# Attention probabilities packed at 80 columns a head, ten full tiles a chunk

## The reference, cut to what matters

```python
Q = (queries @ W_q.T).reshape(b, sq, 16, 16).transpose(0, 2, 1, 3)
K = (keys @ W_k.T).reshape(b, -1, 16, 16).transpose(0, 2, 1, 3)
V = (values @ W_v.T).reshape(b, -1, 16, 16).transpose(0, 2, 1, 3)
scores = jnp.einsum('bhqd,bhkd->bhqk', Q, K) / scale
scores = jnp.where(mask, scores, NEG_INF)
attention = jax.nn.softmax(scores, axis=-1)
heads_out = jnp.einsum('bhqk,bhkd->bhqd', attention, V)
out = heads_out.transpose(0, 2, 1, 3).reshape(b, sq, 256) @ W_proj.T + b_proj
```

## Time and profile before

| what | value |
|---|---|
| median of 3 executions | 1815.34 us (1811.38 to 1818.04) |
| span of the profiled execution | 1817.2 us; its own time beyond the span is not listed, and the three times lie on both sides of it |
| busy: PE, DVE, ACT, POOL | 1666.7, 1496.2, 889.4, 774.7 us (92, 82, 49, 43%) |
| mean granted PE clock | 0.981 of full |
| the 2048 matmuls of `x_av` | 246.2 us busy |
| the 1024 transposes of `prob` | 155.9 us busy |
| weight loads | issued in the first 21 us; ACT first uses the second half of them at 44.96 us |

### The profile page before, as it was taken

The page is one execution under the profiler, slowest core; times in us unless marked ns, Lnnn a source line. Parts: engine busy times, 40 slices in busy tenths (PEclk is TensorE's granted clock), DMA queues, the critical chain, the costliest instruction groups (busy, mean ns, idle before and its releaser), DMA issues.

```text
span 1817.2 us, 36129 instructions
## 1 busy us (share of the span) xinstructions
PE 1666.7 (92%) x12064; PEld 1497.1 (82%) x12064; DVE 1496.2 (82%) x3540; ACT 889.4 (49%) x2351; POOL 774.7 (43%) x809
## 2 busy tenths in 40 slices
PE   3699999999999999999999999999999999999986
PEld 3588888889888888888888988888888888898875
DVE  4778888888888888888888888888888888888652
ACT  2255544455554455555445555444555444555441
POOL 2344444444544444444444454444444444445320
PEclk9899999999999999999999999999999999999887
DMA  4000000000000000000000000000000000000000
GB/s 113 9 9 1 15 15 15 14 14 0 14 14 14 14 14 14 0 14 14 14 14 14 12 2 14 14 14 14 14 0 14 14 14 14 14 10 5 9 7 12
DMA packets 44572, 24.99 MB, mean 14 GB/s; under 512 B 24432, under 2 KB 44528, under 8 KB 44528
## 3 DMA queue, kind: packets, MB, share of 16 engines
q1 hardware_dynamic: 44528, 24.43, 5.1%
HBM read 16.03 MB, written 8.39 MB: 13 GB/s over the span
## 4 chain that ended last, share of the span: by engine, by line
PE 56%; DVE 30%; issue 9%; ACT 4%; DVEq 0%; DMA 0%; SPq 0%; POOL 0%; ACTq 0%; POOLq 0%
PE bank L377 49%; DVE a_conv L809 6%; PE bank L611 4%; DVE x_nmax L942 3%; DVE dve_scrap L252 2%; DVE a_xn L759 2%; PE bank L383 2%; DVE f_xn L759 2%; ACT x_prob L1211 2%; DVE a_E L792 1%; DVE a_stats L746 1%; DVE x_stats L746 1%; DVE f_s L1018 1%; DVE f_th L1013 1%; DVE x_xnT_lo L774 1%
## 5 line engine op out<-in xcount | busy, mean ns | idle before, releaser
L1211 ACT ACTIVATE x_prob<-bank,x_nmax 128x77 f32<-128x77 f32 x1024 | 247.7, 327 | 167.9 <-DVE x_nmax L942 163.7
L377 PEld LDWEIGHTS bank<-x_Vx,x_probT 77*128 77x128 f32 x2048 | 251.6, 193 | 2.9
L377 PE MATMUL bank<-x_Vx,x_probT 77*128 77x17 f32 x2048 | 246.2, 255 | 0.0
L1222 ACT ACTIVATE x_probT<-bank 77x512 f32<-77x512 f32 x256 | 152.4, 595 | 92.0 <-PE bank L611 92.0
L942 DVE TENSOR_REDUCE x_nmax<-bank 128x4 f32<-128x308 f32 x256 | 121.3, 474 | 59.8 <-PE bank L377 58.4
L611 PE MATMUL bank<-ident,x_prob 128*77 128x128 f32 x1024 | 155.9, 275 | 0.4 <-ACT x_probT L1222 0.4
L809 DVE SCALAR_TENSOR_TENSOR a_conv<-a_raw,cw,a_conv 128x256 f32<-128x256 f32 x384 | 156.2, 477 | 0.0
L1306 POOL TENSOR_TENSOR x_rstd<-x_ve,mhalf 128x2 f32<-128x2 f32 x32 | 22.6, 706 | 301.2 <-DVE x_ve L752 301.2
L1330 POOL TENSOR_TENSOR a_Er_lo<-a_E,a_Er_hi 128x512 fp32r<-128x512 f32 x32 | 74.2, 2320 | 142.2 <-ACT a_Er_hi L1114 142.2
L611 PEld LDWEIGHTS bank<-ident,x_prob 128*77 128x77 f32 x1024 | 124.0, 148 | 7.6 <-issue 0.6
L377 PE MATMUL bank<-x_K_bd,x_Q_stack 128*128 128x308 f32 x256 | 98.6, 385 | 15.0 <-ACT x_prob L1211 12.3
(11 more groups left out here) (250 smaller groups left out, 5585.2 us busy)
## 6 DMA issues: line engine op xcount, KB each, us to landing
x<-in_x SPq DMA_DIRECT2D x32, 256.0 KB, 2.9
out<-x SPq DMA_DIRECT2D x32, 256.0 KB, 2.2
ctxT<-in_ctxT SPq DMA_DIRECT2D x32, 77.0 KB, 2.5
keep<-in_mask SPq DMA_DIRECT2D x32, 19.2 KB, 2.6
f_s<-in_fWu SPq DMA_DIRECT2D x2, 256.0 KB, 5.6
a_AT<-in_Wv SPq DMA_DIRECT2D x1, 256.0 KB, 3.8
a_okn<-in_Ws SPq DMA_DIRECT2D x1, 256.0 KB, 3.9
a_qn<-in_Wg SPq DMA_DIRECT2D x1, 256.0 KB, 3.8
```

The costliest lines, as they stand in the source:

```text
L377: return pe.matmul(out, lhsT, rhs, start=start, stop=stop, skip_group_check=True)
L1211: ins = act.activation(prob[:, u % 2, i, :], X0[:, i * S2:(i + 1) * S2], ACT.Exp, scale=-1.0, bias=nmax[:, u % 2, i:i + 1])
L1222: act.activation(probT[:, u % 2].rearrange("p h t -> p (h t)"), X1[0:S2, :], ACT.Copy).then_inc(on.x_pT, 1)
```

## The change

`prob` becomes one tile for a whole chunk, [128, 1280]: 16 heads at a pitch of 80 columns, so that it is ten tiles of 128 columns. The last 3 columns of each head stay zero. A transpose now turns a full 128x128 tile, which holds parts of two or three heads. The ten tiles are done in four groups of 2, 3, 2 and 3, in the places of the four units of a chunk. `x_av` multiplies a transposed tile with a block layout of V, `Vbd`: for each tile up to 3 x 17 columns, a head's V rows standing at the partitions where that head's columns fell, zeros elsewhere. A head that is cut by a tile's edge is summed over two tiles in X2.

`Vbd` (two buffers, one for each row parity) is built from `Vtok`, the plain V that ACT's `x_v` writes, by DMAs from SBUF to SBUF, since rows must change partitions. SP's new step `spread_v` issues twelve a row: one for each piece of heads 0 to 7, with heads 8 to 15 (five tiles on) in the same DMA. The pieces are of 77, 48, 29, 77, 16, 61, 64, 13, 77, 32, 45 and 77 tokens, and each token of a piece is two runs of 64 bytes. `spread_v` waits for `x_v` and for the last `x_av` of the row two before; PE's `x_av` of unit 0 waits for all twelve (`vbd_in`). The zeros and ones of `Vbd` are loaded once, by two more DMAs in the list of the second weights.

The waits of `x_prob` and of the ACT step `x_pt` on PE are fitted to the new buffers.

```diff
+PITCH = 80
+NT = NH * PITCH // P
+GROUPS = (range(0, 2), range(2, 5), range(5, 7), range(7, 10))
+VW = 3 * (HD + 1)
...
-        Vx = sb("x_Vx", [S2, NH, HD + 1])
+        Vtok = sb("x_Vtok", [S2, NH, HD])
+        Vbd = [sb(f"x_Vbd_{i}", [P, NT, VW]) for i in range(2)]
-        prob = sb("x_prob", [P, 2, UH, S2])
-        probT = sb("x_probT", [S2, 2, UH, P])
+        prob = sb("x_prob", [P, NH * PITCH])
+        probT = sb("x_probT", [P, NT, P])
...
+        def pieces():
+
+            found = []
+            for h in range(NH // 2):
+                s = 0
+                while s < S2:
+                    t, p = divmod(h * PITCH + s, P)
+                    n = min(S2 - s, P - p)
+                    found.append((s, n, h, t, p, (h - first_head(t)) * (HD + 1)))
+                    s += n
+            return found
...
+            (Vbd[0][:], a["vones"]), (Vbd[1][:], a["vones"]),
...
+            def spread_v(r):
+                sp.wait_ge(on.x_v, upto(r))
+                if second(r):
+                    sp.wait_ge(on.x_av_ps, upto(two_before(r), NU))
+                dst, src = Vbd[r.parity], Vtok[:].rearrange("s (g h) e -> s g h e", g=2)
+                for s, n, h, t, p, col in V_PIECES:
+                    sp.dma_start(dst[p:p + n, t::NT // 2, col:col + HD], src[s:s + n, :, h, :]).then_inc(vbd_in, 16)
...
                     load_context(ra)
+                if rx is not None:
+                    spread_v(rx)
                 if rf is not None:
                     sp.wait_ge(on.f_y, upto(rf))
...
-                for i in range(UH):
-                    ins = pe.transpose(X1[0:S2, i * P:(i + 1) * P], prob[:, u % 2, i, :], ident[:])
+                for i, t in enumerate(GROUPS[u % QU]):
+                    ins = pe.transpose(X1[:, i * P:(i + 1) * P], prob[:, t * P:(t + 1) * P], ident[:])
...
                 if u == 0:
                     pe.wait_ge(on.x_v, upto(r))
+                    pe.wait_ge(vbd_in, upto(r, V_DMAS))
...
-                for i in range(UH):
-                    h = q * UH + i
-                    ins = mm(X2[:, h * (HD + 1):(h + 1) * (HD + 1)], probT[:, u % 2, i, :], Vx[:, h, :])
+                for t in GROUPS[q]:
+                    h, w = first_head(t) * (HD + 1), tile_heads(t) * (HD + 1)
+                    ins = mm(X2[:, h:h + w], probT[:, t, :], Vbd[r.parity][:, t, 0:w], start=(t == 0),
+                             stop=(t == NT - 1))
...
             def x_v(r):
                 if later(r):
-                    act.wait_ge(on.x_av_ps, upto(before(r), NU))
+                    act.wait_ge(vbd_in, upto(before(r), V_DMAS))
                 act.wait_ge(on.x_v_ps, upto(r))
-                act.activation(Vx[:, :, 0:HD], X2[0:S2, 0:D].rearrange("p (h e) -> p h e", h=NH), ACT.Copy).then_inc(on.x_v, 1)
+                act.activation(Vtok[:], X2[0:S2, 0:D].rearrange("p (h e) -> p h e", h=NH), ACT.Copy).then_inc(on.x_v, 1)
...
-                if u >= 2:
-                    act.wait_ge(on.x_pT_ps, upto(r, NU, u - 1))
+                last = min(q + 2, QU)
+                if c == 1:
+                    act.wait_ge(on.x_pT_ps, upto(r, NU, last))
...
-            pool.memset(Vx[:], 1.0).then_inc(z_ready, 1)
+            pool.memset(prob[:], 0.0).then_inc(z_ready, 1)
```

More of the change, by code:

```diff
@@ L219, in build @@
         st_y = [sem(f"st_y{i}") for i in range(2)]
+        vbd_in = sem("vbd_in")
         w_ready = sem("w_ready")
@@ L247, in loaded, with first_head, tile_heads @@
             return row.half * (16 * n) + 16 * n
+        def first_head(t):
+            return t * P // PITCH
+        def tile_heads(t):
+            return (t * P + P - 1) // PITCH + 1 - first_head(t)
+        def pieces():
[8 more added lines that the diff above has]
+            return found
+        V_PIECES = pieces()
+        V_DMAS = 16 * len(V_PIECES)
         def hold(eng, scrap):
@@ L365, in _ @@
             load_context(Row(last - 1, 1))
-            for rf in (Row(last - 2, 1), Row(last - 1, 0), Row(last - 1, 1)):
+            for rx, rf in ((Row(last - 1, 0), Row(last - 2, 1)), (Row(last - 1, 1), Row(last - 1, 0)),
+                           (None, Row(last - 1, 1))):
+                if rx is not None:
+                    spread_v(rx)
                 sp.wait_ge(on.f_y, upto(rf))
@@ L1204, in x_prob @@
                 act.wait_ge(on.x_max, upto(r, NU, u + 1))
-                if u >= 2:
-                    act.wait_ge(on.x_pT_ps, upto(r, NU, u - 1))
-                else:
-                    if later(r):
-                        act.wait_ge(on.x_pT_ps, upto(before(r), NU, NU - 1 + u))
+                c, q = divmod(u, QU)
+                last = min(q + 2, QU)
+                if c == 1:
+                    act.wait_ge(on.x_pT_ps, upto(r, NU, last))
+                elif later(r):
+                    act.wait_ge(on.x_pT_ps, upto(before(r), NU, QU + last))
                 for i in range(UH):
-                    ins = act.activation(prob[:, u % 2, i, :], X0[:, i * S2:(i + 1) * S2], ACT.Exp, scale=-1.0,
+                    col = (q * UH + i) * PITCH
+                    ins = act.activation(prob[:, col:col + S2], X0[:, i * S2:(i + 1) * S2], ACT.Exp, scale=-1.0,
                                          bias=nmax[:, u % 2, i:i + 1])
@@ L1216, in x_pt @@
                 act.wait_ge(on.x_pT_ps, upto(r, NU, u + 1))
[L1217 to L1222, removed]
+                if u >= QU:
+                    act.wait_ge(on.x_av_ps, upto(r, NU, u + 1 - QU))
+                elif later(r):
+                    act.wait_ge(on.x_av_ps, upto(before(r), NU, QU + u + 1))
+                g = GROUPS[u % QU]
+                act.activation(probT[:, g[0]:g[-1] + 1, :].rearrange("p h t -> p (h t)"), X1[:, 0:len(g) * P],
+                               ACT.Copy).then_inc(on.x_pT, 1)
             def x_ot(r):
@@ L1451, in constants, with ones_columns @@
         "iota8": np.tile(np.arange(NE, dtype=f32), (P, 1)),
+        "vones": ones_columns(),
     }
+def ones_columns():
+    vones = np.zeros((P, NT, VW), np.float32)
+    for h in range(NH):
+        for s in range(S2):
+            t, p = divmod(h * PITCH + s, P)
+            vones[p, t, (h - t * P // PITCH) * (HD + 1) + HD] = 1.0
+    return vones
 def kernel(**inputs):
@@ L1476 @@
     arrays = {f"in_{n}": np.ascontiguousarray(v) for n, v in arrays.items()}
-    nc = bacc.Bacc("TRN2", target_bir_lowering=False, num_devices=1)
+    nc = bacc.Bacc("TRN2", target_bir_lowering=False, num_devices=1, dynamic_dma_scratch_size=1024)
     aps = {n[3:]: nc.dram_tensor(n, v.shape, mybir.dt.from_np(v.dtype), kind="ExternalInput").ap()
```

## The result

The changed kernel took 2066.7 us (median of 4 runs, 2066.3 to 2067.87), the kernel before 1815.01 us beside it: a ratio of 1.139, with an interval of 1.137 to 1.141. I had forecast 1900 us, from 1810 to 1980. The sign and the kind of loss were right; the size was not. The profiled execution has a span of 2064.2 us, 247 us more than before, and a mean granted clock of 0.907 where there was 0.981.

What follows compares the result with a forecast made beforehand. PE bounds the kernel, with DVE leading each pass up to unit 5's scores. 29 full passes at +2.8 us (81) plus 3 for filling and draining took the 1817.2 us span to 1901, median 1900 us; range 1810 to 1980.

Steps and rivals of the forecast that it cites:

- The step that failed: SP's twelve V issues: 0.47 us apart (0.43 to 0.60), eleven steps 5.2 us, V complete at 856.0, PE stalled 3.6 us.
- The second term: PE's work behind unit 5's scores: fewer transposes and matmuls save 2.06 us a pass, and DVE can just follow.
- DVE's five waits: DVE's waits for PE, or ACT behind PE, after unit 5's scores start: 2.4 us, set against PE's saving of 2.06.
- the forecast's mechanism: V late at `x_av` 0; PE's gap drops the clock to 1.2 GHz each full pass, 6.8 us taken; chance 0.6.
- the forecast's +0.2: Full pass with the clock at full: the stall costs 2.25 us, the saving returns 2.06, so +0.2 us.
- my 2.8: Loss per full pass with 6.8 us of low clock: unit 5's scores 4.9 us later, less 2.06 saved, +2.8 us.
- +3: The passes that fill and drain: V's way is less covered, but 3.7 us are saved too; +3 us for three together.
- The clock holds: Rival: the clock stays at full through the stall; 1824 us, 1800 to 1880 over V's landing bounds; chance 0.15.
- V in time: Rival: the twelve transfers complete before PE reaches `x_av` 0, pass 2.4 us shorter, 1745 us; chance 0.06.
- The pieces queue on few engines: Rival: 61- and 29-token pieces each run on one DMA engine, V complete near 859, 1985 us; chance 0.15.

Runs made afterwards that it cites:

- experiment 2: Changed kernel with ACT's `x_v` moved forward to right behind `x_xnt`, all twelve DMAs kept: 1810.01 us, ratio 0.9986 to the kernel before.
- experiment 6: Kernel of experiment 2 with PE's `f_u1` moved in front of the scores of unit 5: 1780.99 us, ratio 0.9823 to the kernel before.
- experiment 4: Changed kernel with `Vtok` padded by three zero rows, so that all DMA pieces are multiples of 16 tokens: 2009.57 us.
- experiment 9: Kernel of experiment 4 with only head `h` in each DMA, two dimensions and half the bytes; heads 8 to 15 get no V: 1995.6 us.
- experiment 1: Changed kernel without its twelve DMAs a row and the wait for them, products with V not computed: 1810.66 us, ratio 0.9992 to the kernel before.
- experiment 3: Changed kernel, V still late, with 64 extra matmuls of 240 columns on PE ahead of the wait for the DMAs: 1973.22 us.
- experiment 8: Changed kernel, V still late, with only every second piece, six DMAs a row; the other blocks of `Vbd` stay empty: 1854.85 us.

## Why the prediction missed

**Right: what the stall is and when PE reaches it.** PE arrives at `x_av` 0 4.1 us behind the end of `x_v` (967.1 - 962.99), where I had 4.0. SP starts 0.1 us behind `x_v`; the last piece lands 974.18 - 972.09 = 2.1 us behind the start of its issue, the value that I took. The packets hide (experiment 2). The new forms come at the old spacing: 984.50 - 984.17 = 0.33 us for three transposes (0.11), and six matmuls at 991.26 that are followed at 991.84, 0.097 us each where I had 0.101. The sums that I named for a full clock, 154 and 100 us, came out at 170.9 and 113.0 in experiment 6: a group of three transposes is 0.49 us busy at a spacing of 0.11, one of two 0.38, so each group carries some 0.16 us beside its spacing, and the groups are shorter now.

**The step that failed: "SP issues one DMA after another at 7.65 - 7.17 = 0.48 us; I take 0.47, as its addresses are fixed."** The step measured (972.09 - 963.10) / 11 = 0.82 us, outside the bounds of 0.43 and 0.60. Eleven steps are 9.0 us instead of 5.2, and V was complete 11.2 us behind the end of `x_v`, not 7.6: 3.6 us later. PE's stall was 7.08 us, not 3.6. My bounds came from loads and a store, none of which has SBUF on both sides, an odd count of partitions or three dimensions; I had weighed the odd counts for the landing alone. Experiments 4 and 9 split the 0.35 us: 0.16 for the counts, 0.03 for the third dimension with half of the runs, and 0.16 for what is left of the form.

**The second term: "It can, just."** I let DVE give PE the whole saving of 2.06 us behind unit 5's scores. From those scores to `x_out` it was 882.02 - 861.55 = 20.47 us, and is 1004.53 - 985.05 = 19.48: only 0.99 came through. PE's `a_ot` now waits 0.38 us for POOL's `a_o`, and its `a_wo` 0.36 us for DVE's `a_oT_lo`, which stands behind the 3.35 us of the reciprocal `a_rC`. I had set DVE's five waits against the saving as one sum of 2.4 us, but 1.6 us of them (0.95 and 0.68 before, [0.90] and [0.72] after) are waits for PE's last products, where they stay whatever PE saves. These rows of DVE before are the two waits that the earlier trace rows does not show, one of them left out of my sum:

```profile
862.52 0.69 DVE L815 SCALAR_TENSOR_TENSOR a_qkv<-a_qkv,a_conv 128x512 f32<-128x512 f32 x1 [0.24 <-ACT a_qkv L1130]
...
870.67 0.48 DVE L942 TENSOR_REDUCE x_nmax<-bank 128x4 f32<-128x308 f32 x1 [0.16 <-PE bank L377]
```

With the 0.19 and 0.40 of the earlier trace rows they make 1.0 us, of which 0.2 is left after; the one other long wait, 1.52 us for ACT's `a_okn`, is as long as before. So DVE had hardly more to give than what came through. This is read from the trace; I did not move `a_rC` to test it. Experiment 1's undisturbed passes agree: 52.5 against 53.5.

**The clock.** That it would fall in every full pass was the forecast's mechanism, and it does. I took 6.8 us at 1.2 GHz; it is 10.2 us, of which 7.8 lie on work. In the sum the clock's part was 2.8 - 0.2 = 2.6 us, and experiment 3 measured 3.0. The Trainium skill ("TensorE: Matmul & The Clock Gate", section "HAM oscillation — how this bites in real kernels") describes just this: a wait for a DMA in each turn of a loop, and a cold stretch that is paid anew in each turn. This trace agrees, with 3.0 us of 61.5 in each.

**The sum again.** With a held clock: the forecast's +0.2, 3.6 for the later V and 1.07 for the saving that did not come through make +4.9; experiment 3's passes are 58.45 - 53.5 = +4.95. The clock adds 3.0: +7.9, the measured 61.4. Of the 5.1 us a pass by which this exceeds my 2.8, 3.6 are the issues, 1.1 the saving that DVE did not let through and 0.4 the clock. Over 29 passes 7.9 us are 229; measured are 220 between the full passes and 8 behind the last of them, where the distance between two `x_v` grew from 50.9 to 58.9. The rest of the 247, 19 us, is at the ends, where I had +3: the first distance grew from 48.8 to 61.0 and the last from 49.5 to 53.4, and 3 us lie ahead of the first `x_v` and behind the last. The first and the last two rows have a DMA wait of 6.8 to 8.3 us, with a low clock around it.

**The rivals.** *The clock holds:* refuted by the windows, in all 29 passes. *V in time:* refuted in this kernel, and its price was wrong too: experiment 2 is that rival, with V complete before PE comes, and gave 1810 us, not 1745. Of the 2.4 us a pass that it was to gain, 1.0 is there when the clock holds, and the clock then falls in about every second pass. *The pieces queue on few engines:* its 1985 us is nearer to the result than my own number, for a reason that isn't the one seen. The last piece lands 2.1 us behind its issue, and nothing queues. The Trainium skill's rule that I put beside that rival ("DMA: Bandwidth & Descriptors", section "Why a DMA increments its semaphore by 16 and not by 1") does show, but in the issue: pieces for which it gives 16 engines or one (48, 16, 32; 29, 61) took 0.64 to 0.71 us, those for which it gives 11, 13 or 15 (77, 13, 45) took 0.84 to 0.90. The 64 tokens right behind the 61 are an exception, with 0.81 us; they took 0.63 in experiment 4, where all are multiples of 16, and 0.67 in experiment 8, behind the 16. That the number of engines is what an issue pays for is argued from this, not shown. That the rule sets the number of engines here is borne out by the packet counts of the queue in experiments 1, 4, 8 and 9:

```profile
q1 hardware_dynamic: 44816, 24.95, 5.1%
...
q1 hardware_dynamic: 91920, 27.60, 6.0%
...
q1 hardware_dynamic: 66768, 26.22, 5.5%
...
q1 hardware_dynamic: 71440, 26.29, 5.4%
```

The changed kernel has 88656 - 44816 = 43840 packets more than the one without the twelve DMAs, 1370 a row: 1232 are the runs, and the other 138 are what the rule's engines for the twelve pieces add up to (four times 11, four times 16, twice 1, 13 and 15). The other three counts come out to the packet in the same way.

The Trainium skill's rule for weight loads ("TensorE: Matmul & The Clock Gate", section "LDWEIGHTS (loading the stationary operand)"), by which the wider transposes would save nothing, was not borne out for the narrow ones: it gives 0.107 us for 128 columns and 0.064 for 77. The spacing is 0.108 us at both widths, and the loads last 148 ns in the mean at both, before and in experiment 6. The products with V, whose loads have 128 columns too, come at 0.097.

## What to carry to other kernels

Price a chain of small DMAs by its issues, and take the price from issues of the same form (source, count of partitions, dimensions); if the trace has none, the range must reach well past the nearest row (here 0.82 us a step against 0.48). Then ask where the producer can move: here one step moved in ACT's order hid all twelve. And when PE gets less work in a part of the loop that another engine leads, look at the gap that this makes: filled with work that is there anyway it kept the clock up, and only then did the saving of the packed tiles, 1.3%, reach the time.

## What the runs showed of the hardware

- An SP issue of a DMA from SBUF to SBUF with 64-byte runs took 0.59 to 0.66 us in nearly all cases where every count is a multiple of 16 (experiments 4 and 9), and 0.84 to 0.90 us in the changed kernel for 77, 45 and 13 tokens, in most passes the same within 0.02 us for the same place in the list. The plain loads took 0.43. It does not grow with the tokens: 13 took 0.88, 48 took 0.64.
- 384 such DMAs cost no time where they had 18 us to land in. Their packets are 43840 of the 88656 - 44528 = 44128 that came on top of the kernel before; 288 belong to the two loads at the start.
- A PE gap of 1.5 us in each pass was followed by a lower clock in 12 of 29 passes, one of 2.2 us in 16, ones of 5.2 and 7 us in all. Two waits of 0.65 and 0.69 us, 1.3 us apart, were followed by one in 3 of 29 (the kernel before). Each stretch lasted 3.4, 6.8 or 10.2 us.
